# Convolution input copied out of its PSUM bank, one tap a round; matrix units shared out evenly to the last round; weight loads, start-up units and idle products moved

## What is computed

```python
xn = _layernorm(x, axis=-1)
x = x + _L0_attn_ref(xn, ...) + _L0_ffn_ref(xn, ...)

# _L0_attn_ref: a state space layer, in spite of its name
u = xn @ W_in + b_in                       # 256 -> 512 channels
u = depthwise_causal_conv(u, conv_w) + conv_b    # 4 taps along the rows
h = tanh(A) @ h + u_t * Bp;  y = Cp . h + Dp * u_t   # scan over the rows
out = silu(y) @ W_out + b_out

# _L0_ffn_ref: attention with 16 heads of 16, and 8 experts, of which each row takes its top 2
attn = softmax(q k' / 4) v
moe  = sum over 8 experts of (xn @ W_experts[e] + b_experts[e]) * combine[:, e]
```

## Time and profile before

| | |
|---|---|
| median of 3 runs | 901.84 us (900.23 to 904.38) |
| the profiled execution: its time, its span | 906.3 us, 904.5 us |
| busy: PE, DVE, ACT, POOL | 802.3, 559.1, 512.9, 366.5 us |
| score of step 0, of step 11 | at 29.6, at 92.5 us |
| score of step 240 (the plan's last M units are in step 238) | at 833.8 us |

### The profile page before, as it was taken

The page is one execution under the profiler, slowest core; times in us unless marked ns, Lnnn a source line. Parts: engine busy times, 40 slices in busy tenths (PEclk is TensorE's granted clock), DMA queues, the critical chain, the costliest instruction groups (busy, mean ns, idle before and its releaser), DMA issues.

```text
span 904.5 us, 12976 instructions
## 1 busy us (share of the span) xinstructions
PE 802.3 (89%) x4324; PEld 453.2 (50%) x4324; DVE 559.1 (62%) x834; ACT 512.9 (57%) x884; POOL 366.5 (41%) x524
## 2 busy tenths in 40 slices
PE   6468997899989999989989998999988998999775
PEld 4235664555545564546545554456545554555221
DVE  4274665585567757785577746695767657574530
ACT  3223654565656666566456755666556654566443
POOL 4243552554235443455145513455245522445000
PEclk9686999999999999999999999999999999999756
DMA  3901010112111121112111121012111111112100
GB/s 107 241 1 28 10 37 12 25 37 73 46 36 37 32 79 25 28 30 83 37 37 37 37 71 30 20 36 83 37 37 36 37 48 25 25 37 60 36 2 24
DMA packets 32386, 39.68 MB, mean 44 GB/s; under 512 B 8433, under 2 KB 18455, under 8 KB 32320
## 3 DMA queue, kind: packets, MB, share of 16 engines
q1 hardware_dynamic: 31262, 36.94, 15.8%
q0 software_dynamic: 384, 1.12, 0.5%
q10 hardware_dynamic: 674, 0.80, 0.3%
HBM read 8.90 MB, written 4.59 MB: 15 GB/s over the span
## 4 chain that ended last, share of the span: by engine, by line
PE 71%; DVE 19%; issue 6%; ACT 1%; DMA 1%; SPq 1%; POOL 0%; ACTq 0%; POOLq 0%; DVEq 0%
PE PS L386 37%; PE SB L511 11%; DVE mx L923 10%; PE PS L541 9%; PE TB L525 5%; DVE ys L777 4%; PE PS L436 3%; PE PS L402 2%; DVE ys L773 1%; DVE qkl L803 1%; DVE xl L809 1%; PE PS L409 1%; PE PS L483 1%; PE PS L398 1%; PE PS L470 1%
## 5 line engine op out<-in xcount | busy, mean ns | idle before, releaser
L923 DVE TENSOR_REDUCE mx<-SB 128x2 f32<-128x1024 f32 x256 | 313.4, 1224 | 252.4 <-PE SB L511 251.9
L976 POOL TENSOR_TENSOR acc<-acc,mt 128x256 f32<-128x256 f32 x320 | 235.8, 743 | 264.6 <-ACT mt L577 203.7
L708 ACT ACTIVATE Pt<-TB 128x1024 f32<-128x1024 f32 x256 | 262.6, 1026 | 99.2 <-PE TB L525 97.9
L577 ACT ACTIVATE mt<-PS,cpad 128x256 f32<-128x256 f32 x256 | 107.4, 471 | 128.0 <-PE PS L386 127.3
L511 PE MATMUL SB<-kst,qst 48*128 48x512 f32 x512 | 133.0, 516 | 30.6 <-DVE mx L923 26.6
L541 PE MATMUL PS<-Pt,V 128*17 128x512 f32 x1024 | 143.0, 632 | 1.1 <-ACT Pt L708 1.1
L386 PE MATMUL PS<-weh,xTh 128*128 128x512 f32 x256 | 115.0, 449 | 22.2 <-DVE ys L777 21.1
L511 PEld LDWEIGHTS SB<-kst,qst 48*128 48x128 f32 x512 | 49.4, 190 | 138.5 <-DVE mx L923 71.4
L525 PE MATMUL TB<-qst,kst 50*128 50x512 f32 x512 | 109.7, 424 | 8.2 <-ACT Pt L708 4.3
L386 PE MATMUL PS<-wel,xTh 128*128 128x512 f32 x256 | 105.4, 412 | 0.0
L386 PE MATMUL PS<-weh,xTl 128*128 128x512 f32 x256 | 105.0, 410 | 0.0
(11 more groups left out here) (144 smaller groups left out, 1106.4 us busy)
## 6 DMA issues: line engine op xcount, KB each, us to landing
qst<-qkh SPq DMA_DIRECT2D x126, 64.0 KB, 2.2
kst<-qkh SPq DMA_DIRECT2D x126, 64.0 KB, 2.2
out<-acc SPq DMA_DIRECT2D x8, 512.0 KB, 2.9
kst<-qkl SPq DMA_DIRECT2D x63, 64.0 KB, 2.2
qst<-qkl SPq DMA_DIRECT2D x63, 64.0 KB, 2.2
acc<-in_x SPq DMA_DIRECT2D x7, 512.0 KB, 3.9
Bt<-in_wexp SPq DMA_DIRECT2D x2, 512.0 KB, 6.1
raw<-in_wexp SPq DMA_DIRECT2D x2, 512.0 KB, 6.3
```

The lines of the kernel that those rows point to most:

```text
L577: return e.activation(mt[:, item % NM, :], P, ACT.Copy, scale=scale)
L708: e.activation(Pt[:, T % NP, :, :], TB[:, :, :], ACT.Exp, scale=0.25).then_inc(s_ex, 1)
L923: e.tensor_reduce(mx[:, g % 2, 0:2, 4 * jj + a], SB[:, :, :], AX.X, ALU.max).then_inc(s_mx, 1)
L976: e.tensor_tensor(v, v, mt[:, item % NM, :], ALU.add).then_inc(s_mt, 1)
```

## The change

`conv` no longer reads the bank. ACT copies a Y unit to a new SBUF buffer `uc` (two deep), which frees the bank, and DVE does one tap a step from there, taps 0 to 3 in four steps, each right after `largest`. Tanh, product and parts follow two steps later than before, and an O unit may come 9 steps after its Y instead of 7. `Pt` goes from four buffers to three; W_out is staged in `uc`.

`plan()` has no fixed budget any more: in each step it takes the work still left, divided by the steps still left up to `STEPS + LAG - 3`, that is 264. `WANTED` and some bounds of `soonest` are other numbers. M units of a batch may wait, so that in the new plan the last batch's M units are in steps 244 to 263, and each step from 11 to 263 holds about the same. In the start-up Q0.2 and Q0.3 come in step 1, ahead of G in step 2; Z in step 4, the four B in 5 and 6, the first Y in 7; four M units (before: six) precede step 11, but the T and two V units of batch 1 do too.

W_in, one expert weight (W_E2) and W_out are loaded ahead of the stacks; W_E3 comes after batch 1. The response product (`cpc`) comes after Q0.1 instead of V0.0. PE gets products of the identity that nobody reads: 5 before the Krylov products, one behind each of six of these, 10 at the end of step -1. `store` has its own step for each batch (`store_at`).

```diff
-NP = 4
+NP = 3
-WANTED.update({("M", i): 2 * i - 7 for i in range(16)})
+WANTED.update({("M", i): 2 * i for i in range(16)})
...
-        return max(after(("Y", b, i // 2 * 2 + 1), 7), after(("C", b, 0), 1))
+        return max(after(("Y", b, i // 2 * 2 + 1), 9), after(("C", b, 0), 1))
+    def fixed(t):
+        pairs = (0 <= t < STEPS) + (LAG <= t < STEPS + LAG)
+        return 0.45 * pairs + 1.05 * (LAG + 2 <= t < STEPS + LAG + 2 and (t - LAG) % 2 == 0)
+    last, spent = STEPS + LAG - 3, 0.0
     for t in range(END):
         row = steps[t]
-        spent = min(spent, 0.0) + (STEP_US if t >= 32 else 3.7) - (0.9 if t < LAG else 0.5 if t >= STEPS else 0.95)
-        if t > LAG and (t - LAG) % 2 == 0 and t < STEPS + LAG + 2:
-            spent -= 1.05
+        left = sum(COST[u[0]] for u in todo) + sum(fixed(n) + (COST["X"] + COST["P"]) / 8 for n in range(t, last))
+        spent = min(spent, 0.0) + left / max(last - t, 1) - fixed(t)
...
-            if kind == "Y":
-                free[bank] = u.read + 1
-            elif kind == "Z":
+            if kind == "Z":
...
+            def idle_turns(n):
+                for _ in range(n):
+                    e.matmul(OB[:, 0:128], ident[:, :], ident[:, :], start=True, stop=True)
+            e.wait_ge(s_id, 2)
+            e.wait_ge(s_init, 1)
+            idle_turns(5)
             for s in range(6):
                 krylov(s)
+                idle_turns(1)
...
+                if t == -1:
+                    idle_turns(10)
...
+                elif u.kind == "Y":
+                    n = 4 * b + i
+                    if n >= 2:
+                        e.wait_ge(s_cv, 4 * n - 4)
+                    else:
+                        e.wait_ge(s_lo[W_OUT], 4)
+                    e.copy(uc[:, i % 2, :], P[:, :]).then_inc(s_free[u.bank], 1)
...
-                for b, d in y_read(t - 1):
-                    conv(b, d, (2, 3))
+                for s in range(4):
+                    for b, d in y_read(t - s - 1):
+                        conv(b, d, s)
...
-                elif u.kind == "Y":
-                    return conv(b, i, (0, 1))
...
+            for w in (W_IN, W_E2, W_OUT):
+                load_w(w)
             half_stack(e, 0, 0, s_st[0])
             stack(1)
-            for w in (W_IN, W_E2, W_E3, W_OUT):
-                load_w(w)
             load_x(1)
+            load_w(W_E3)
             load_x(2)
```

More of the change, by code:

```diff
@@ L56, in soonest @@
         if kind == "T":
[L57 removed]
+            return max([ln.get(b, END) + 5, 7] + [after(("M", b - 2, n), 1) for n in range(16) if b >= 2])
         if kind == "V":
[L59 removed]
+            return max(after(("T", b, 1), 1), 32 * b - 18 if b > 1 else 0)
         if kind == "Q":
[L61 removed]
+            return max(after(("T", b, 1), 1), 32 * b - 10 if i < 2 else 32 * b + 6 if b else 1)
         if kind == "G":
@@ L163, in late, with store_at @@
     return AT[t][:-1] if t in AT else []
+def store_at(b):
+    return max(UNIT["P", b, 4 * b + 3].read + 1, UNIT["M", b, 15].read + 2, UNIT["O", b, 3].read + 2)
 def gate_count(b, name):
@@ L580, in unit @@
                 P, b, i = FB[u.bank], u.b, u.i
-                if u.kind in "PYG" or u.kind == "Z" and i == 0:
+                if u.kind in "PG" or u.kind == "Z" and i == 0:
                     return
@@ L755, in split @@
                     e.tensor_tensor(lo, stg, F(hi), ALU.subtract).then_inc(s_lo[w], 1)
[L757 to L774, removed]
-                    else:
-                        e.wait_ge(s_cv, 3 * n + s)
-                        ins = e.scalar_tensor_tensor(out=y[:, s:512], in0=P[:, 0:512 - s], scalar=cwc[:, d, 3 - s:4 - s],
-                                                     in1=y[:, s:512], op0=ALU.mult, op1=ALU.add)
-                    ins.then_inc(s_free[u.bank] if s == 3 else s_cv, 1)
@@ new lines, in conv @@
+            def conv(b, d, s):
+                y, v, n = ys[:, d % 2, :], uc[:, d % 2, :], 4 * b + d
+                if s == 0:
+                    e.wait_ge(*freed("Y", b, d))
+                    if n >= 2:
+                        e.wait_ge(s_y, n - 1)
+                    else:
+                        e.wait_ge(*full("G", 0, 0))
+                        e.wait_ge(s_Rl, 1)
+                        if n == 0:
+                            e.wait_ge(s_c[C_CW], 16)
+                    if b == 0:
+                        e.wait_ge(*freed("B", 0, d))
+                    ins = e.scalar_tensor_tensor(out=y, in0=v, scalar=cwc[:, d, 3:4], in1=Bt[:, d, :],
+                                                 op0=ALU.mult, op1=ALU.add)
+                else:
+                    e.wait_ge(s_cv, 4 * n + s)
+                    ins = e.scalar_tensor_tensor(out=y[:, s:512], in0=v[:, 0:512 - s], scalar=cwc[:, d, 3 - s:4 - s],
+                                                 in1=y[:, s:512], op0=ALU.mult, op1=ALU.add)
+                ins.then_inc(s_cv, 1)
@@ L1150, in _ @@
                     max_row(g)
-                b, rest = divmod(t - LAG - 35, 32)
-                if rest == 0 and 0 <= b < NB:
-                    store(b)
-                    if b + 3 < NB:
-                        e.wait_ge(s_out, 16 * b + 16)
-                        load_x(b + 3)
+                for b in range(NB):
+                    if t == store_at(b):
+                        store(b)
+                        if b + 3 < NB:
+                            e.wait_ge(s_out, 16 * b + 16)
+                            load_x(b + 3)
             e.wait_ge(s_out, 16 * NB)
```

58 lines of the change are left out of this document (28 added, 30 removed).

## The result

The changed kernel takes 835.87 us (median of 4 runs, 831.45 to 839.47) against 903.11 us of the kernel before in the same runs: a ratio of 0.925, with a 95% interval of 0.919 to 0.932. The forecast was 845 us, with a range of 827 to 872. The profiled execution has a span of 836.7 us, 67.8 us less than the one before; the sum of the forecast had 57.8.

The account below looks back on a forecast made before the run. PE was taken to bound the middle, with both ends at less busy PE and lower clock. Span 904.5 - 17.8 (start) - 17 (middle) - 23 (tail) = 846.7 us; timed forecast 845 us, range 827 to 872.

Parts of the forecast that it names:

- Start: -17.8 forecast: Steps up to 11: step 11's score starts at 74.7 instead of 92.5 us; bounds 5 and 24 us.
- Nearest is the row of 4.1 us, so G starts at 39.0: Start: `Rraw`, issued at 34.81, lands after 4.1 us like an earlier 383.5 KB DMA, so G starts at 39.0.
- the upper bound of 42.0: Start: latest landing forecast for `Rraw`, as before, at 42.0 us; the lower bound was 38.9.
- rival 2: Start bound elsewhere: `Rraw` no earlier, DVE delays Z; only 5 of 17.8 us gained, total 858; chance 0.12.
- a first B at 51.5: Start: B needs `srs`, DVE's row copy plus five SP DMAs, moved with G by 3 us to 51.5.
- Middle and tail: -40 forecast: Steps 11 to 263: 757 us, 40 less; middle -17 (bounds 0, -27), tail -23 (bounds -14, -26).
- two thirds of the 24.7 us behind the taps: Middle: PE's waits behind convolution taps holding a bank (L777) lose their cause; two thirds booked, -17 us.
- the signs named beforehand: Step 11 at 74 to 76, G at 39, no tap waits, PE's clock near full until step 263, among others.
- signs of being wrong: PE waits behind the maximum above 30 us, step 11 later than 85, or a middle over 3.1 us a step.
- Rival 1: Middle: the maximum, ACT's M copies or blocked taps take over the wait behind L777; total 861; chance 0.17.
- Rival 3: Each of 128 taps waits 0.6 us for POOL, holding up `largest` and `score`: 77 us, total 922; chance 0.03.
- on the path I put 0: Taps from SBUF cost DVE 10 us more, counted as 0 because DVE waits for PE a third of the time.

Follow-up runs that it names:

- the run with units to step 245: Changed kernel with the even share of units reaching only to step 245 instead of 263, steps 246 to 263 with only the spine: 871.34 us.
- the runs that moved DVE's time: Two variants of the changed kernel: an extra maximum behind each tap, 868.65 us; POOL's additions replaced by a tiny memset, 829.54 us.

## Why the prediction was right, by its own steps

**Start: -17.8 forecast, -10.1 measured.** The step that failed is "Nearest is the row of 4.1 us, so G starts at 39.0". G started at 43.94, even behind the upper bound of 42.0 that I had given. Nothing came earlier there, for two reasons. The first I had priced at nothing, the second I had left to rival 2. The idle products behind the Krylov products don't lie in gaps: the Krylov products now follow each other every 0.99 us (before: 0.66), and the whole chain to the stacks and to kd starts 1.0 to 1.6 us later (the run without them shows it). And the loads that stayed behind the stacks, 1.5 MB, were enough to hold `Rraw` as long as 3 MB had: 7.5 us, against 3.0 with none. That is 4.9 of the 7.7 us by which step 11 is late. The later terms were near: G to Z 7.2 us (forecast 6.9), Z 6.5 (5), from the end of Z to score 7 8.8 us (9.1), steps 7 to 10 15.9 us (14.7; score 7 at 66.48, score 11 at 82.35). How the forecast came from DVE's copy of the row to a first B at 51.5 can't be followed from its rows; B did start right behind Z and score 5. The 10 idle products delayed no score by themselves; PE idled another 3.46 us for the stacks.

**Middle and tail: -40 forecast, -56.7 measured.** The mechanism was right, the size not. I booked two thirds of the 24.7 us behind the taps and kept the rest of the idle time and all of the low clock. Idle time between step 11 and 263 was forecast at 33 us and is 740.5 - 714.0 = 26.5 us; work at full clock is 714.0 x 0.99 = 707 us (forecast 709), so low clock costs 7 us, not 15 (the 0.99 is rounded, which leaves some 3 us either way). The third that I kept back was not kept: PE's waits for taps went from 24.7 to 0 and came back as 31.5 when the bank was held again. What I had not seen is that an even plan helps the middle too, shown by the run with units to step 245. The bounds were too narrow as well: alone, the copy took 37.0 us off (my bound was 27, which is more than the 24.7 us of waits that it was drawn from) and the even plan 29.9 (bound 26), and the two together more than the 53 of both bounds.

**The sum** came within 9 us partly by luck. The start brought 7.7 us less than forecast, the middle and tail 16.7 more, and the two misses have opposite signs. Of the signs named beforehand, the missing waits behind taps and the full clock up to step 263 came true; step 11 at 74 to 76, G at 39, the first B at 51 to 52, idle time near 33 us and taps of 0.68 to 0.82 us did not. None of the signs of being wrong came.

**Rival 1** (the wait changes its name) did not happen to a size that matters: the wait behind the maximum is 16.7 us, less than the 20.2 of the same steps before. **Rival 2** (start bound elsewhere) was half of what happened, since `Rraw` did land no earlier. **Rival 3** (blocked taps) is real in its mechanism and small in its sum. The taps are blocked by 0.19 to 0.21 us on average instead of 0.08, and by the runs that moved DVE's time (0.38 and 0.3 us a us) these 26 us cost 8 to 10 us of the total, an estimate, where I had put 0. That is the second sentence of the forecast that was wrong: "on the path I put 0", since a DVE that waits for PE a third of the time is not a cover for all it does.

**Tail.** As forecast: every step to 263 full, clock at 1.00, and the last 13.9 us much as they were (14.8).

## What to carry to other kernels

A PSUM bank that is read by a chain of slow steps is worth one more copy on an engine with room: 32 copies of 0.59 us took some 27 to 37 us off here, even though they made the chain itself slower. When a schedule fills one engine, share the work out over all steps to the last one; that saves the light steps at the end and gives every other step slack for its waits. And an engine with 30% of idle time can still be on the path: add a known amount of work to it and see what share comes through, before calling its time free.

## What the runs showed of the hardware that was not expected

- A read of 320 KB from DRAM took 6.3 to 7.5 us in seven runs with 1.5 MB of other loads issued just before it (7.1 with 3 MB), 4.0 when it was issued 1.4 us ahead of these loads, and 3.0 to 4.4 in the three runs in which they had gone out long before. Here what crosses a small transfer on the critical path about doubles its time.
- The taps, DVE instructions with both inputs in SBUF, took 0.93 to 0.96 us on average beside POOL's additions, up to 1.76 us for one, and 0.743 us (tap 0) with these additions gone. So with POOL out of the way tap 0 is as quick from SBUF as from PSUM (0.744), and not quicker. The Trainium skill ("SBUF — State Buffer", Who interferes with whom) says that a DVE instruction with two SBUF inputs contends with a GpSimd instruction that reads SBUF. The traces agree, and put the average at 0.2 us for an instruction of 0.74 us with POOL busy 45% of the time. Whether it is the reads of the additions or their writes, no run tells.
- Idle products ahead of and between small dependent products won nothing here. PE's matmuls doubled their rate at 19.3 us in the changed kernel's trace, at 22 to 28.3 us in the seven other traces with the same idle products, and at 17.1 and 17.0 in the two without any. The run without was 6.1 us faster by its median.
- The granted clock of a window reads 1.00 where the trace holds no record of it. PE's matmuls went at half rate for 4 to 13 us in windows from 15 to 28 us that read 1.00. In the start the level is read from the time of a known matmul (0.43 us from start to start for 512 columns, or 0.23), not from the window.
